# The attention's output projection placed later in TensorE's order, ahead of the state's update

## What is computed

```
x = x + attn_a(layernorm(x))     # gated linear attention, then a GELU MLP, with its own residuals
x = x + ffn(layernorm(x))        # 8 experts 256x256, top 2
x = x + attn_b(layernorm(x))     # recurrence h = tanh(x B + h A^T), 16 states, then C and W_out
x = x + ffn(layernorm(x))        # the same experts
```

```
S = exp(gt) * S + kt vt^T        # state per head, token by token
o = qt S
x = x + (rms(o) * silu(g)) @ Wo  # the output projection
x = x + gelu(ln(x) @ W1 + b1) @ W2 + b2
```

## Time and profile before

| | us |
|---|---|
| median of 3 runs | 1946.68 |
| lowest, highest | 1942.38, 1947.51 |
| the profiled execution | 1937.87 |
| its span, first to last instruction | 1936.1 |

### The profile page before, as it was taken

The page is one execution under the profiler, slowest core; times in us unless marked ns, Lnnn a source line. Parts: engine busy times, 40 slices in busy tenths (PEclk is TensorE's granted clock), DMA queues, the critical chain, the costliest instruction groups (busy, mean ns, idle before and its releaser), DMA issues.

```text
span 1936.1 us, 47586 instructions
## 1 busy us (share of the span) xinstructions
PE 1796.5 (93%) x16264; PEld 1553.0 (80%) x16264; DVE 1310.4 (68%) x3877; ACT 917.7 (47%) x2534; POOL 1121.6 (58%) x1453
## 2 busy tenths in 40 slices
PE   2588899999999999999999999999999999999887
PEld 1467788888888888888888888888888888887765
DVE  2566577777776777777767777777677777765443
ACT  2344455555444545554445455545455554453321
POOL 1666567556666666566667665665675565654211
PEclk9688899999999999999999999999999999999888
DMA  3110000000000000000000000000000000000000
GB/s 115 38 30 23 23 23 19 27 16 27 27 27 22 26 18 27 16 27 27 27 22 22 22 22 22 27 27 27 22 18 25 19 25 28 23 24 4 3 12 11
DMA packets 71883, 47.79 MB, mean 25 GB/s; under 512 B 37616, under 2 KB 71056, under 8 KB 71696
## 3 DMA queue, kind: packets, MB, share of 16 engines
q1 hardware_dynamic: 70368, 45.41, 7.8%
q10 hardware_dynamic: 1456, 1.59, 0.2%
HBM read 30.21 MB, written 16.78 MB: 24 GB/s over the span
## 4 chain that ended last, share of the span: by engine, by line
PE 69%; POOL 17%; ACT 4%; issue 4%; DVE 3%; POOLq 0%; DMA 0%; ACTq 0%; DVEq 0%; SPq 0%
PE ps L956 50%; PE ps L973 8%; POOL sx L434 8%; PE ps L962 3%; PE ps L981 2%; POOL r L348 2%; PE ps L983 2%; POOL osq L430 1%; POOL stage L450 1%; PE ps L1013 1%; PE ps L1018 1%; DVE yT L780 1%; PE ps L993 1%; POOL ra L348 1%; POOL ra L370 1%
## 5 line engine op out<-in xcount | busy, mean ns | idle before, releaser
L956 PE MATMUL ps<-we,yT 128*128 128x512 f32 x3072 | 843.4, 414 | 3.5 <-DVE yT L780 2.2
L956 PEld LDWEIGHTS ps<-we,yT 128*128 128x128 f32 x3072 | 554.5, 193 | 106.2 <-DVE yT L780 7.9
L487 ACT ACTIVATE hs<-ps 16x8 f32<-16x8 f32 x1024 | 177.8, 174 | 836.4 <-PE ps L973 830.0
L973 PEld LDWEIGHTS ps<-hs,aT 128*128 128x128 f32 x2048 | 352.3, 195 | 120.1 <-issue 68.4
L973 PE MATMUL ps<-hs,aT 128*128 128x8 f32 x2048 | 331.4, 236 | 51.8 <-ACT hs L487 50.0
L376 POOL TENSOR_TENSOR part<-part 128x256 f32<-128x256 f32 x64 | 47.4, 741 | 418.1 <-ACT part L505 418.1
L728 DVE SCALAR_TENSOR_TENSOR stage<-ps,coef,stage 128x256 f32<-128x256 f32 x384 | 185.1, 482 | 143.6 <-POOL stage L378 114.7
L434 POOL TENSOR_TENSOR sx<-osq,cst 32x512 f32<-32x512 f32 x128 | 214.8, 1678 | 10.0
L728 DVE SCALAR_TENSOR_TENSOR acc<-ps,coef,acc 128x256 f32<-128x256 f32 x384 | 184.9, 482 | 23.9 <-POOL acc L378 10.5
L399 POOL TENSOR_TENSOR orstd<-omean,mhalf 128x32 f32<-128x32 f32 x32 | 174.1, 5439 | 2.7
L780 DVE TENSOR_TENSOR yT<-ps,yT 128x512 fp32r<-128x512 f32 x64 | 44.0, 691 | 116.6 <-ACT yT L662 67.9
(11 more groups left out here) (172 smaller groups left out, 3504.8 us busy)
## 6 DMA issues: line engine op xcount, KB each, us to landing
xin<-in_x SPq DMA_DIRECT2D x64, 128.0 KB
vrow<-vtok SPq DMA_DIRECT2D x32, 256.0 KB, 2.1
vx<-vrow SPq DMA_DIRECT2D x128, 64.0 KB, 2.0
xag<-in_x SPq DMA_DIRECT2D x64, 128.0 KB
out<-stage SPq DMA_DIRECT2D x64, 128.0 KB
stage<-in_experts SPq DMA_DIRECT2D x1, 2048.0 KB, 7.8
stage<-in_Wvg SPq DMA_DIRECT2D x1, 512.0 KB, 4.2
stage<-in_W SPq DMA_DIRECT2D x1, 512.0 KB, 6.1
```

The source lines that it names most:

```text
L487: return a.activation(hs[0:N, :, k], bt(ps[0:N, BANK["RB"], 0:TOK])[:, :, k], ACT.Tanh)
L956: ins = t.matmul(dst, left(lp, c), right(rp, c), start=(n == 1), stop=(n == 3 * chunks))
L973: return t.matmul(bt(ps[0:NP, BANK["RB"], 0:TOK])[:, :, k], aT[:], hs[:, :, (k - 1) % TS], start=False, stop=True, skip_group_check=True)
```

## The change

The block of WO moves in TensorE's body from between the transposes of `kt` and step 0 to between step 3 and `state_update(0)`. Its last matmul now counts a semaphore `WO`, and VectorE waits for it ahead of the sum `xmid`.

```diff
--- before.py
+++ after.py
@@ -861,6 +861,7 @@
                                          eq[:, :, TS - 1:TS].rearrange("p (i q) o -> p i q o", q=BQ).broadcast_to([P, TILES, BQ, HQ * DV]),
                                          ALU.mult).then_inc(sem("dstate"), 1)
                 if live(it, 3):
+                    dve.wait_ge(sem("WO"), c3)
                     v.tensor_tensor(xmid[:].rearrange("p i d -> p (i d)"), ps[:, BANK["WO"], :], xhat[:].rearrange("p i d -> p (i d)"), ALU.add).then_inc(sem("xmid"), 1)
                     dve.wait_ge(sem("xmid"), c3)
                     stats(xmid, st_f, mv_f, "f", c3)
@@ -1209,13 +1210,6 @@
                     for i in range(TILES):
                         ins = t.transpose(ps[:, BANK["KT"], i * P:(i + 1) * P], kt[:, i * P:(i + 1) * P], ident)
                     ins.then_inc(sem("KT"), 1)
-                if live(it, 3):
-
-                    for name, count in readers(it, "WO"):
-                        pe.wait_ge(sem(name), count)
-                    for i in range(TILES):
-                        ins = product(ps[:, BANK["WO"], i * D:(i + 1) * D], lambda p, c: oTs[:, p, c, i * P:(i + 1) * P],
-                                      lambda p, c: wcols(W_O, p, c, D, 0, D), KC)
                 if live(it, 5):
                     recur(0).then_inc(sem("rnn_mm"), 1)
                 if live(it, 2):
@@ -1252,6 +1246,14 @@
                     pe.wait_ge(sem("weights"), WEIGHTS)
                     pe.wait_ge(sem("rnn_h"), target)
                     recur(3).then_inc(sem("rnn_mm"), 1)
+                if live(it, 3):
+
+                    for name, count in readers(it, "WO"):
+                        pe.wait_ge(sem(name), count)
+                    for i in range(TILES):
+                        ins = product(ps[:, BANK["WO"], i * D:(i + 1) * D], lambda p, c: oTs[:, p, c, i * P:(i + 1) * P],
+                                      lambda p, c: wcols(W_O, p, c, D, 0, D), KC)
+                    ins.then_inc(sem("WO"), 1)
                 if live(it, 2):
 
                     target = value(pe, c2)
```

## The result

The changed kernel is slower. Its median over 22 runs is 1946.7 us (1943.6 to 1961.0), against 1940.9 us (1930.4 to 1947.5) over 22 runs of the kernel before. The ratio is 1.0054, with a 95% interval of 1.0037 to 1.0070, so about 6 us lost (0.5%) and clear of 0.3%. The profiled executions show more: a span of 1957.0 us against 1936.1. The chain that ended last was followed through both, and each profile was cut into fill, 25 full rounds and drain, at the starts of `emid` (in all profiles after the first, the cuts lie up to 0.2 us beside them).

The account below looks back on a forecast made before the run. GpSimd and ScalarE bound the kernel from `emid` to the recurrence's step 7, TensorE from there to the next `emid`. 0 + 0 - 5.7 (clock) - 0.6 (drain) = -6.3 us, from 1946.68 to 1940.4; range 1932 to 1950.

Parts of the forecast that it names:

- The idle time and the length of a round: TensorE's wait before the recurrence's step 7 grows from 1.25 us to 1.4; full-clock rounds stay at 55.3 us.
- the 0.15 us of the recurrence's round trip: Between recurrence steps 3 and 4: the projection covers the stall, 0.15 us a round, taken as 0, other bound 3.8 us.
- The new wait: VectorE's wait for the projection ahead of `xmid`: met when reached, cost 0, under 0.1 us a round as other end.
- `gTs`: VectorE's input to the feed-forward's second product: still ready 0.67 us before the product's earlier start, cost 0.
- `ktok`: Waits on ScalarE behind the recurrence's tanh 0, so it comes earlier by as much as step 0; cost 0.
- the sooner second product: Feed-forward's second product comes 1.46 us earlier for VectorE, but GpSimd takes up that root only later: nothing gained.
- The old stretch: Small TensorE work, 2.7 us, before the clock's fall; wide product put in its middle should stop falls, up to 6.35 us.
- the first rival: Falls move under the second product, behind output product, `kt`'s transposes, step 0, first scores, step 1: 2 to 16 us; chance 0.12.
- The 5.7 us taken for the clock: Gain from fewer clock falls in loop and drain: three quarters of 7.65 us.
- The drain: First drain round: projection between recurrence steps 3 and 4 covers a bare round trip, 0.6 us saved.
- The rule on idle gaps: Skill lays TensorE's clock falls to idle gaps between matmul bursts; by it the change saves no clock, 1946.1 us.
- the second rival: TensorE's clock falls as often as before, or places only trade: -0.6, 1946.1 us; chance 0.26 together with half gone.

Follow-up runs that it names:

- `y0` first: The changed kernel with VectorE normalising `y0` ahead of `att` instead of behind it: 1930.6 us, against 1944.6 of the kernel before (0.9946); measured again, 1935.0 us (0.9991).

## Why the prediction was wrong

The forecast was 6.3 us less; measured were 5.9 us more (1946.7 against 1940.9). That 1946.7 is a time between 1932 and 1950 is luck: the three runs from which the forecast started had a median of 1946.7, 5.8 above that of all 22.

**The idle time and the length of a round: right.** The first scores start 5.4 us behind `emid` instead of 6.8. VectorE waits 1.13 us for the second product, 1.0 expected. Rounds at full clock stay at 55.3. Idle time before step 7 is 1.26 us, not 1.4: the 0.15 us of the recurrence's round trip were won (steps 3 and 4 start 2.12 us apart, 1.54 of them the projection's, against 0.74 before), but the projection took up 1.54 us at its new place and had freed only 1.39 at the old one. It made no difference.

**The new wait, `gTs`, `ktok`, the sooner second product: right,** at 0.

**Where the falls go: the wrong case was taken as the likeliest.** The old stretch did lose its falls, all of them. But the first rival's stretch, 2.74 us by the rows, got 10 or 11 in their place, against 8 to 11. I gave that 0.12 because the output product has 256 columns, and because matmuls on a quarter of the array had kept the clock at 1.00. Two stretches of the same length, made of the same kind of small matmuls, should have been given much nearer chances; the rows named did not tell them apart by anything that a run had shown to matter. The 5.7 us taken for the clock were 0 or less.

**The price of a fall there: the term that was mis-sized.** The first rival priced a fall of 3.4 us at 0.3 (1.7 less the slack of 1.4). Measured, 1.8. Ten of them make 18 instead of 3; less the 6.35 us of the old falls that is +11.7, and the loop lengthened by 11.8 (1401.1 - 1389.3). At the rival's own price the moved falls would have left the loop some 3 us shorter, so it is this term that turned the sign. The working held the slack before step 7 to be the only thing behind the second product. It left out the other end of the same stretch: `DS1`, `att`, `y0`, `dstate`, `xmid`, `yT`, and the bank that the transposes need. `y0` started 1.36 us ahead of GpSimd's long operation, and 1.5 us later it was caught behind it, which cost it 1.5 us more. Where a loop here delays it, it is by 1.4 us or more, so at what delay the price sets in is not shown. The statement that a wait for `gTs` of up to 1.25 us would vanish in the idle time left out the same path; what such a wait would have cost, no run shows. With `y0` first the price was 0.3, just the figure of the rival: 1.5 us late less 1.25 of idle time.

**The drain: not -0.6.** The projection does cover one round trip there: from the recurrence's input product to the expert product behind step 5 the round took 9.80 us before and 10.94 after, of which 1.52 are a fall under the second product, so 0.4 us were saved. But that fall took the place of the one under the expert product, and in the two profiles the drain is 232.0 and 221.2 us, against 226.2 and 227.7 before, with mean clocks of 0.85 and 0.91 against 0.89 and 0.88. I can't read 0.6 us in that. The fill, taken at 0, was 324.0 and 319.6 us against 320.5 and 321.3.

**The rule on idle gaps** (The Trainium skill, TensorE: Matmul & The Clock Gate, "HAM oscillation"): the second rival, that nothing would change, was wrong too. In the 20 us ahead of any fall of the loop TensorE was idle for 0.06 us at most, in every run.

**What stays open.** The loop loses 12 to 15 us in profiles, the runs' medians only 6 to 8.5. So some 6 us come back in fill and drain, as in the second profile, whose drain was 5 to 6.5 us shorter than the two of the kernel before. Which of the changes brings that about, or whether it is the place of the loop's end against the clock's falls, was not found. What of the small matmuls brings the clock down, and why in 6 to 12 rounds of 25 and not in all, is open as well.

## What to carry to other kernels

Slack has to be worked out for each reader of a late result, not for the engine: here the engine had 1.25 us to spare, but a VectorE instruction in the middle was done only 0.63 us before GpSimd's long operations began, and once it is caught behind them it pays what is left of them on top of the delay. When wide products keep a row of small matmuls apart, moving one joins two stretches; lay the joined stretch beside one in the same kernel behind which the clock is known to fall before you count on a gain. And the cure may be small: here the order of two VectorE instructions gave 11 us against the changed kernel measured beside it, and between 0 and 14 against the kernel before.

## What the runs showed of the hardware

- The granted clock fell to 0.50 behind 2.7 us of small matmuls on 16 or 32 rows, transposes and recurrence steps with next to no idle time (0.06 us at most in the 20 us ahead), in 6 to 12 of 25 rounds a place; one product of 12 matmuls of 128x256 (1.5 us) in such a stretch prevented it in every round of the loop, one of 6 did not.
- VectorE's fp32 `tensor_scalar` on SBUF (two of 128x256) takes 0.73 us alone and 2.2 to 2.5 us if it starts at most 0.3 us behind a GpSimd `tensor_tensor` of 1.04 us that is followed by one of 1.3 us; 1.36 us if it starts 0.4 us behind a single one of 1.28. The other way round GpSimd's 1.28 us became 1.39 to 1.45. A `tensor_tensor` with one input in the PSUM kept its 0.68 us beside the one of 1.04.
- Two profiles of one kernel gave drains of 221.2 and 232.0 us, at a mean granted clock of 0.91 and 0.85.
